# One core, a post-norm transformer block of two layers: the last eight rows of weighted values are summed on TensorE, constants load in two groups, and all engines get another order

## The reference

```python
x = L0_attn_x                                           # (32, 256, 128)
x = _layernorm(x + _L0_attn_ref(x, ...))                # A: 16 heads of 8, softmax(q k / sqrt 8 - slope |i - j|) v
x = _layernorm(x + _L0_ffn_ref(x, ...))                 # B: 8 experts (top 2) and a shared one, silu(x w1) * (x w3) @ w2
x = _layernorm(x + _L1_attn_ref(x, ...))                # C: below
x = _layernorm(x + _L1_ffn_ref(x, ...))                 # D: 8 experts (top 2), one matrix each
```

```python
for off in OFFSETS:
    scores.append(einsum('bhnd,bhnd->bhn', q, shift(k, off)) * scale)
attn = softmax(stack(scores, -1) + pos_bias, -1)
for i, off in enumerate(OFFSETS):
    out = out + attn[..., i:i + 1] * shift(v, off)      # the weighted values and their sum
gate = sigmoid(x @ w_gate + b_gate)
return (out * gate) @ w_out + b_out
```

## Time and profile before

| | |
|---|---|
| median of three runs | 1625.95 us |
| the profiled execution | 1623.99 us |
| its span | 1622.2 us |
| PE busy | 1416.7 us, 87% |
| DVE busy | 1360.9 us, 84% |
| ACT busy | 910.1 us, 56% |
| POOL busy | 740.9 us, 46% |
| mean granted clock of TensorE | 0.969 |

### The profile page before, as it was taken

The page is one execution under the profiler, slowest core; times in us unless marked ns, Lnnn a source line. Parts: engine busy times, 40 slices in busy tenths (PEclk is TensorE's granted clock), DMA queues, the critical chain, the costliest instruction groups (busy, mean ns, idle before and its releaser), DMA issues.

```text
span 1622.2 us, 34112 instructions
## 1 busy us (share of the span) xinstructions
PE 1416.7 (87%) x11872; PEld 1082.2 (67%) x11872; DVE 1360.9 (84%) x3774; ACT 910.1 (56%) x1836; POOL 740.9 (46%) x644
## 2 busy tenths in 40 slices
...
GB/s 170 91 86 131 121 107 101 128 134 123 95 127 134 100 101 128 135 124 92 128 132 102 101 127 133 105 107 134 113 102 114 134 122 88 119 92 87 77 45 39
DMA packets 83560, 179.69 MB, mean 111 GB/s; under 512 B 9771, under 2 KB 65835, under 8 KB 66219
## 3 DMA queue, kind: packets, MB, share of 16 engines
...
## 4 chain that ended last, share of the span: by engine, by line
DVE 39%; PE 39%; issue 10%; ACT 6%; DMA 2%; POOL 2%; SPq 1%; DVEq 0%; ACTq 0%; POOLq 0%
PE bPV L518 8%; DVE mneg L998 7%; DVE nDy L938 5%; PE bTU L547 4%; PE b L556 4%; DVE wb L900 4%; PE bTU L548 4%; DVE wb L961 3%; DVE gc L862 3%; ACT x L727 3%; PE bS L535 3%; PE b L421 2%; PE bTU L465 2%; DVE gat L979 2%; PE bTU L480 2%
## 5 line engine op out<-in xcount | busy, mean ns | idle before, releaser
L998 DVE TENSOR_REDUCE mneg<-bS 128x2 bf16<-128x512 f32 x512 | 342.2, 685 | 68.1 <-PE bS L538 68.1
L1058 POOL TENSOR_TENSOR wb<-wb 128x1024 f32<-128x1024 f32 x64 | 150.4, 2350 | 524.2 <-DVE wb L900 524.2
L1066 POOL TENSOR_TENSOR prod<-kC,qC 128x512 f32<-128x512 f32 x256 | 367.4, 1470 | 17.5 <-ACT kC L658 17.3
L696 ACT ACTIVATE sil<-bTU,b 128x256 f32<-128x256 f32 x288 | 133.2, 474 | 327.4 <-PE bTU L548 227.7
L686 ACT ACTIVATE P<-bTU 128x512 f32<-128x512 f32 x512 | 280.3, 597 | 32.9 <-PE bTU L482 32.3
L1078 POOL TENSOR_TENSOR h<-ub,gBcb 128x256 f32<-128x256 f32 x256 | 182.8, 727 | 248.9 <-DVE ub L1011 214.5
L535 PE MATMUL bS<-stack 96*128 96x256 bf16 x1024 | 225.7, 279 | 32.0 <-DVE mneg L998 25.8
L480 PE MATMUL bTU<-stack 97*128 97x256 bf16 x1024 | 214.0, 277 | 17.3 <-ACT P L686 15.3
L538 PE MATMUL bS<-dist,identh 128*128 128x128 f16 x1024 | 200.7, 223 | 0.0
L482 PE MATMUL bTU<-dist,identh 128*128 128x128 f16 x1024 | 194.2, 221 | 0.0
L547 PE MATMUL bTU<-x1T,w 128*128 128x256 f32 x576 | 181.0, 396 | 2.0 <-DVE ub L1011 2.0
...
## 6 DMA issues: line engine op xcount, KB each, us to landing
...
```

Source lines behind the costliest of these rows:

```text
L998: v.tensor_reduce(mneg[:, :, k], bS[k % 2][:].rearrange("p (a b) -> p a b", a=TT), op=ALU.max, axis=AX.X, negate=True).then_inc(dveS.done( ...
L1066: tt_(prod[:, 2 * p:2 * p + 2, :], shifted(kC, p), qC[:].unsqueeze(1).to_broadcast([128, 2, T]), ALU.mult).then_inc(poolC1.done("prod", p), 1)
```

## The change

**The sum of the weighted values.** GpSimd's two adds stay. The three adds of VectorE go. A new step `C2.sm` on TensorE adds the remaining eight rows in PSUM, with the identity as the weights and the eight rows as moving data, in a bank of the rotation, which now has 30 members instead of 29. Its first four matmuls wait for `C2.add.0` and the other four for `C2.add.1`. `C2.gt` reads that bank.

**The constants.** Four constants and bv0 that pass 0 needs are loaded first (`ld_first`); the scores' constants follow, and the other 19 transfers stand behind `A1.rows.2` of pass 0. TensorE waits for them ahead of pass 1, and the tables are made on VectorE and ScalarE behind pass 1.

**The order** of all five engines is written anew.

```diff
 ORDER = {
     "pe": """
-        B2.z A1.qk S.s.0 A1.v A2.ST.0 A2.ST.1 S.s.1 S.s.2 A2.ST.2 A2.ST.3 A2.ST.4 S.s.3 S.s.4 A2.ST.5 A2.ST.6
...
+        A1.qk S.s.0 S.s.1 B2.z A2.ST.0 S.s.2 S.s.3 A2.ST.1 A1.v A2.ST.2 A2.ST.3 S.s.4 A2.ST.4 S.s.5 A2.ST.5 A2.ST.6
+        A2.PV.0 A2.ST.7 A2.ST.8 S.s.6 B.xT A2.ST.9 S.s.7 A2.ST.10 D.xT A2.PV.1 A2.ST.11 B.lg A2.ST.12 D.lg C1.xT
+        S.s.8 A2.ST.13 C1.qk A2.PV.2 A2.ST.14 A2.ST.15 D.y.0 S.s.9 D.y.1 C1.vg C2.sm B.cT S.s.10 B.ab.0 B.ab.1
...
     "pool": """
-        B.h.2 B.h.3 B.h.4 B.h.5 A3.xbo B.h.6 B.h.7 C2.xb B.h.8""",
+        C2.add.0 C2.add.1 C1.prod.0 C1.prod.1 C1.prod.2 C1.prod.3 C1.prod.4 C1.prod.5 C1.prod.6 C1.prod.7 A3.xbo
+        C2.xb B.h.1 B.h.2 B.h.3 B.h.4 B.h.5 B.h.6 B.h.7 B.h.8""",
     "sp": """
-        C2.wb A1.part.0 A1.part.1 X.xT A3.x A1.part.2 B.cT A1.rows.0 B.cb A1.rows.1 A1.rows.2 D2.out C1.dw M.m C1.wb""",
+        C2.wb A1.part.0 D2.out A1.part.1 A1.part.2 X.xT B.cT A3.x A1.rows.0 B.cb A1.rows.1 A1.rows.2 C1.dw M.m C1.wb""",
...
-        turn = [(what[-2:], n) for what, n in ORDER["pe"] if what in ("A2.ST", "B.ab", "D.y")]
+        turn = [(what[-2:], n) for what, n in ORDER["pe"] if what in ("A2.ST", "B.ab", "D.y", "C2.sm")]
...
             sp.dma_start(xT[:], A["xT"][:, 0:T]).then_inc(ld_xT, 16)
-            for dst, name in consts:
-                sp.dma_start(dst[:], A[name]).then_inc(ld_const, 16)
...
+            for dst, name in first_consts:
+                sp.dma_start(dst[:], A[name]).then_inc(ld_first, 16)
...
+                    if t == 0 and (what, n) == ("A1.rows", 2):
+                        for dst, name in consts:
+                            sp.dma_start(dst[:], A[name]).then_inc(ld_const, 16)
...
         def _(pe):
             mm = nc.tensor.matmul
-            pe.wait_ge(ld_const, 16 * N_CONST)
-            pe.wait_ge(setup_dve, SETUP_DVE)
-            pe.wait_ge(setup_act, SETUP_ACT)
+            pe.wait_ge(ld_first, 16 * N_FIRST)
...
+                if t == 1:
+                    pe.wait_ge(ld_const, 16 * N_CONST)
+                    pe.wait_ge(setup_dve, 12)
+                if t == LAG["C1"]:
+                    pe.wait_ge(setup_dve, SETUP_DVE)
+                    pe.wait_ge(setup_act, SETUP_ACT)
...
+                    if what == "C2.sm" and (e := r["C2"]) is not None:
+                        take(turn_bank("sm", 0), ("C2", dveC2, "gt", 0), t)
+                        o = bTU[turn_bank("sm", 0)]
+                        for p in range(2):
+                            pe.wait_ge(poolC2.sem, poolC2.count(e, "add", p))
+                            for x in range(4):
+                                i = mm(o[:, 0:T], ident[:], pv[:, 8 * p + x, :], start=(p == 0 and x == 0),
+                                       stop=(p == 1 and x == 3))
+                        i.then_inc(peC2.done("sm"), 1)
...
-                        v.tensor_tensor(pv[:, 0:4, :], pv[:, 0:4, :], pv[:, 8:12, :], ALU.add).then_inc(dveC2.done("add", 0), 1)
...
-                        v.tensor_tensor(pv[:, 0:2, :], pv[:, 0:2, :], pv[:, 2:4, :], ALU.add).then_inc(dveC2.done("add", 1), 1)
...
-                        v.tensor_tensor(pv[:, 0, :], pv[:, 0, :], pv[:, 1, :], ALU.add).then_inc(dveC2.done("add", 2), 1)
                     if what == "C2.gt" and (e := r["C2"]) is not None:
-                        dve.wait_ge(dveC2.sem, dveC2.count(e, "add", 2))
+                        dve.wait_ge(peC2.sem, peC2.count(e, "sm"))
                         dve.wait_ge(actC1.sem, actC1.count(e, "g"))
                         dve.wait_ge(peC2.sem, peC2.count(e - 1, "out"))
-                        v.scalar_tensor_tensor(gat[:], tg[:], 1.0, pv[:, 0, :], ALU.add,
+                        v.scalar_tensor_tensor(gat[:], tg[:], 1.0, bTU[turn_bank("sm", 0)][:, 0:T], ALU.add,
...
+                if t == 1:
+                    tables()
             passes(one)
```

More of the change, by code:

```diff
@@ L60 @@
     "dve": """
-        B2.res D2.mom N.root.0 S.max.0 A1.rest N.root.1 S.max.1 S.max.2 N.root.2 A1.v N.root.3 S.max.3 A1.mid A1.lo
-        C2.pv.0 C2.pv.1 C2.pv.2 C2.pv.3 S.max.4 S.max.5 S.max.6 G.rank C2.pv.4 C2.pv.5 C2.pv.6 C2.pv.7 G.weigh
-        S.max.7 S.max.8 C2.add.0 D.acc.0 C2.add.1 D.acc.1 S.max.9 B.wu.0 B.wu.1 C2.add.2 S.max.10 C2.gt B.wu.2
-        D.acc.2 S.max.11 A3.rec S.max.12 C2.res A3.num S.max.13 B.wu.3 B.wu.4 B.wu.5 C1.mx S.max.14 S.max.15 B.wu.6
-        C1.sum B.wu.7 B.wu.8 A3.res D.acc.3""",
+        S.max.0 S.max.1 B2.res D2.mom S.max.2 N.root.0 S.max.3 N.root.1 N.root.2 S.max.4 N.root.3 S.max.5 A1.rest
@@ L66 @@
+        C2.pv.0 C2.pv.1 C2.pv.2 C2.pv.3 A1.v A1.mid S.max.6 S.max.7 G.rank C2.pv.4 A1.lo C2.pv.5 C2.pv.6 C2.pv.7
+        G.weigh D.acc.0 S.max.8 D.acc.1 C2.gt S.max.9 S.max.10 B.wu.0 B.wu.1 S.max.11 D.acc.2 B.wu.2 C2.res S.max.12
+        S.max.13 A3.rec B.wu.3 A3.num S.max.14 B.wu.4 C1.mx B.wu.5 S.max.15 B.wu.6 C1.sum A3.res B.wu.7 B.wu.8
+        D.acc.3""",
     "pool": """
-        C2.add.0 C2.add.1 C1.prod.0 C1.prod.1 C1.prod.2 C1.prod.3 C1.prod.4 C1.prod.5 C1.prod.6 C1.prod.7 B.h.1
-        B.h.2 B.h.3 B.h.4 B.h.5 A3.xbo B.h.6 B.h.7 C2.xb B.h.8""",
+        C2.add.0 C2.add.1 C1.prod.0 C1.prod.1 C1.prod.2 C1.prod.3 C1.prod.4 C1.prod.5 C1.prod.6 C1.prod.7 A3.xbo
@@ L216, in network @@
         peC1 = steps("peC1", "xT qk vg sc scT wT")
-        peC2 = steps("peC2", "out")
+        peC2 = steps("peC2", "sm out")
         peD = steps("peD", "xT lg y*4")
@@ L233, in network @@
         dveC1 = steps("dveC1", "mx m2 sub subo sum rec w")
-        dveC2 = steps("dveC2", "pv*8 add*3 gt")
+        dveC2 = steps("dveC2", "pv*8 gt")
         dveC2n = steps("dveC2n", LN)
@@ L772, in _, with tables @@
-            v.tensor_tensor(oobE[:], oobE[:], oobm[:], ALU.add).then_inc(setup_dve, 1)
-            dve.wait_ge(setup_dve, SETUP_DVE)
+            dve.wait_ge(ld_first, 16 * N_FIRST)
+            dve.wait_ge(setup_dve, 12)
+            def tables():
+                dve.wait_ge(ld_const, 16 * N_CONST)
+                v.tensor_reduce(posm[:], posd[:], op=ALU.max, axis=AX.X).then_inc(setup_dve, 1)
+                v.tensor_reduce(oobm[:], oobd[:], op=ALU.max, axis=AX.X).then_inc(setup_dve, 1)
+                dve.wait_ge(setup_dve, 14)
+                v.tensor_tensor(posd[:], posd[:], posm[:].unsqueeze(2).to_broadcast([128, 2, DUP]),
+                                ALU.subtract).then_inc(setup_dve, 1)
+                v.tensor_tensor(oobd[:], oobd[:], oobm[:].unsqueeze(2).to_broadcast([128, H, len(OOB)]),
+                                ALU.subtract).then_inc(setup_dve, 1)
+                dve.wait_ge(setup_act, 6)
+                v.tensor_reduce(poss[:], posd[:], op=ALU.add, axis=AX.X).then_inc(setup_dve, 1)
+                v.tensor_reduce(oobs[:], oobd[:], op=ALU.add, axis=AX.X).then_inc(setup_dve, 1)
+                dve.wait_ge(setup_act, 8)
+                v.tensor_tensor(posE[:], posE[:], posm[:], ALU.add).then_inc(setup_dve, 1)
+                v.tensor_tensor(oobE[:], oobE[:], oobm[:], ALU.add).then_inc(setup_dve, 1)
+                dve.wait_ge(setup_dve, SETUP_DVE)
```

78 lines of the change are left out of this document (33 added, 45 removed).

## The result

The changed kernel takes 1641.53 us (median of 10 runs, 1635.37 to 1646.07), the kernel before 1627.89 beside it (10 runs, 1624.51 to 1634.74). The ratio is 1.0076, 95% interval [1.0054, 1.0099]: slower by 0.8%, where 1651 had been forecast from a median of 1625.95 (1.5%).

A forecast was written before the change was run, and what follows sets the result against it. TensorE was taken as the limit, with 45.0 us of work a pass after the change. +30 us over 27 passes, 0 for constants and -4 at the end gave a span of 1648, forecast 1651 us, range 1637 to 1664.

The forecast's parts named there:

- the forecast's own range: Whole kernel: 1637 to 1664 us around 1651, the pass to within 0.5 us, chance 0.63.
- TensorE's floor of 45.0 us a pass: Full passes: 41.6 us of TensorE work plus 3.4 for eight new matmuls makes 45.0 us.
- The cast held by GpSimd's add: A1.mid on VectorE, held until GpSimd's first add ends: about 2.4 us, and S.s.8 on TensorE waits 1.3 us.
- the choice between two bounds: A1.mid beside GpSimd's add: cost 0 if it runs through, 2.1 us of VectorE if held; the upper was taken.
- rival 1: GpSimd doesn't hold the cast, S.s.8 does not wait, pass 46.2 us: 1615 to 1621 us in all, chance 0.25.
- The stalls of 0.5 at B2.z and 0.5 at S.s.4 and S.s.5: TensorE early in a full pass: waits of 0.5 us at B2.z, 0.1 at S.s.4 and 0.4 at S.s.5.
- B2.z "needs B.h.8": TensorE behind S.s.1: B2.z must wait for B.h.8, which ends near 2.0 us, a stall of 0.5 us.
- The constants: Start of the run: S.s.0 2.4 us earlier, lost again to late parts and tables; net 0, bounds -8 and +5.
- The last passes: From 1500 us on: GpSimd's products at 1.28 us each without VectorE's adds beside them, -4 us in all.
- What the sum is worth: Full passes: the sum adds 3.4 us to TensorE's floor; VectorE, without the adds, has some 4 us to spare.

The follow-up runs named there:

- experiment 1: Changed kernel with only the cast A1.mid moved on VectorE, ahead of the four first products, directly behind A1.rest: 1579.39 us, ratio 0.9691 to the kernel before.
- Experiment 3: Kernel before with only A1.mid and A1.lo moved on VectorE behind the first four products, as in the changed kernel: 1677.98 us, ratio 1.0312.
- experiment 4: Kernel before with only the constants loaded in two groups and the tables made behind pass 1: 1629.55 us, ratio 0.9993.
- Experiments 5 to 7: Kernel before with the sum on TensorE alone (1.0617); changed kernel with VectorE's three adds instead of the sum, cast late (1.0570) and early (1.0206).

## Why the prediction was right, and where it was not

The direction held, and 1641.5 lies inside the forecast's own range, 9.5 us below its middle. In part that is luck. The change by the medians is +13.6 us, about half of the +25 forecast; the traces have +21.5, since the two executions read lie on opposite sides of their medians, and two errors in the pass cancel. Step by step:

- **TensorE's floor of 45.0 us a pass.** Right: a pass of 45.09 where the waits are gone (experiment 1). TensorE's busy time of 45.00 is inside the forecast's 45 to 46; VectorE's is 40.2 against 39.
- **The cast held by GpSimd's add.** Right: 2.46 us against 2.4 forecast, and S.s.8 waits 1.15 by the record, 1.3 by the matmuls' pitch. This was the choice between two bounds, and rival 1 fell with it. The rule cited there from the Trainium skill ("SBUF — State Buffer", section "SBUF: two separate sides") agrees here for a cast too. Experiment 3 shows the other side: the cast that starts 0.16 us ahead of GpSimd's add is not stretched, and the add takes 2.47 us instead of 2.35.
- **The stalls of 0.5 at B2.z and 0.5 at S.s.4 and S.s.5.** Wrong: TensorE's idle time is 1.4 us a pass, all but the wait at S.s.8 in gaps of 0.2 and less. B2.z starts at 808.54 directly behind S.s.1. The step failed on the sentence that B2.z "needs B.h.8": it waits expert by expert, and the ninth is needed only for its last two matmuls (four records), 1 us later. B.h.8 ends 2.1 us after the start of the pass, as forecast. VectorE comes to B2.res at 3.2 instead of 3.7, and the stalls at S.s.4 and S.s.5 are gone with that.
- **The clock.** A term that the sum did not have. 20 of 26 passes lose 1.6 us to half clock behind the wait, +1.2 in the mean. The mean pass is 47.5 us, the 47.45 of the forecast, only because the 1.0 us of stalls that did not come and the 1.2 of clock that was left out cancel: luck. The passes together are +27.1 against +30. The signs were in the trace of before: at 943 and 1271 us its pass is 49.6 us with 6.8 us at half clock, behind the same waits as in the others, and the forecast read only a stretch at 1.00.
- **The constants.** Net 0 was right (experiment 4), its working was not: S.s.0 was to start 2.4 us earlier and does 0.2 earlier, so there was no gain for the losses to eat up. The second group is issued from 19.5 us on instead of 18.5, and its last transfer lands 5.4 us after its issue (28.2 to 33.6) where 3.67 was taken. The 2.6 us that the changed kernel is ahead at pass 5 are not the constants': with them alone pass 5 starts at 147.2, before at 147.0. What brings them stays open.
- **The last passes.** -3.0 against -4, products of 1.27 us against 1.28.
- **What the sum is worth.** The sentence that failed most leaves no trace in the total: the sum is priced as 3.4 us on TensorE's floor, and VectorE's relief only as time "to spare". Experiments 5 to 7 say otherwise for this order. Without the sum, and with the adds where they were tried, it is slower than the kernel before by 5.7%, since the adds, stretched beside GpSimd's products, stand between two row maxima that TensorE waits for. In the changed kernel the sum brings 4.7% back, and what is left as a loss is the place of one cast.
